# Two fully masked attentions on three-bank rings, every second unit in turned order

## What is computed

```python
# L3_attn: 16 heads of 8, 256 queries, 256 keys
attn = jnp.einsum('bhqd,bhkd->bhqk', q, k) * scale
attn = jnp.where(mask, attn, jnp.float32(-jnp.inf))
attn = jax.nn.softmax(attn, axis=-1)
out = jnp.einsum('bhqk,bhkd->bhqd', attn, v)
# L3_xattn: 16 heads of 8, 256 queries, 512 keys of the context
scores = jnp.einsum('bhqd,bhkd->bhqk', query, key_) / jnp.sqrt(D_K)
scores = jnp.where(mask == 0, NEG, scores)
attn = jax.nn.softmax(scores, axis=-1)
ctx = jnp.einsum('bhqk,bhkd->bhqd', attn, value)
```

## Time and profile before

| | us |
|---|---|
| median of 3 runs | 1503.12 (1502.01 to 1513.15) |
| the profiled execution, whole | 1489.0 |
| its span, first to last instruction | 1486.8 |
| TensorE, VectorE, ScalarE, GpSimd busy | 1200.8, 902.3, 704.1, 274.2 |
| mean granted TensorE clock, as a share of full speed | 0.885 |

### The profile page before, as it was taken

The page is one execution under the profiler, slowest core; times in us unless marked ns, Lnnn a source line. Parts: engine busy times, 40 slices in busy tenths (PEclk is TensorE's granted clock), DMA queues, the critical chain, the costliest instruction groups (busy, mean ns, idle before and its releaser), DMA issues. The chain is left out here.

```text
span 1486.8 us, 26544 instructions
## 1 busy us (share of the span) xinstructions
PE 1200.8 (81%) x9482; PEld 739.3 (50%) x9489; DVE 902.3 (61%) x2363; ACT 704.1 (47%) x1344; POOL 274.2 (18%) x549
## 2 busy tenths in 40 slices
PE   4878998687596398567999999999957679878883
PEld 2333334585243298355666666666647633333332
DVE  5747774433677445685776766766741266567746
ACT  3754774121452022212665665665714335526663
POOL 2412110353010255100000000000006513211110
PEclk9886989798799699776999999999988879969995
DMA  7321233494702466100000000000037632212100
GB/s 185 93 55 39 63 94 136 152 289 141 188 2 92 144 226 228 33 1 0 1 1 1 1 1 1 1 2 1 1 91 219 193 118 79 58 28 61 40 2 15
DMA packets 87892, 114.33 MB, mean 77 GB/s; under 512 B 10946, under 2 KB 67983, under 8 KB 87295
## 3 DMA queue, kind: packets, MB, share of 16 engines
q1 hardware_dynamic: 83314, 103.52, 23.5%
q0 software_dynamic: 4448, 9.12, 2.2%
HBM read 85.79 MB, written 25.82 MB: 75 GB/s over the span
## 5 line engine op out<-in xcount | busy, mean ns | idle before, releaser
L870 DVE TENSOR_REDUCE mx<-ps 128x4 f32<-128x1024 f32 (+1 forms) x128 | 153.9, 1221 | 58.3 <-PE ps L794 57.3
L1023 PE MATMUL ps<-probs,vaug 128*32 128x256 f32 (+1 forms) x1792 | 148.4, 406 | 15.2 <-ACT probs L989 8.6
L2508 DVE CUSTOM_DVE_ANT_0 wring<-ps,probs 128x768 f32<-128x768 f32 x128 | 122.6, 958 | 56.9 <-PE ps L2380 56.8
L2464 ACT COPY qs<-ps 128x768 f32<-128x768 f32 x128 | 102.4, 801 | 97.6 <-PE ps L2387 97.6
L979 ACT ACTIVATE probs<-ps 128x1024 f32<-128x1024 f32 x96 | 98.4, 1024 | 77.9 <-PE ps L843 77.5
L984 ACT ACTIVATE probs<-ps 128x512 f32<-128x512 f32 x192 | 106.6, 595 | 45.3 <-PE ps L937 43.6
L243 POOL TENSOR_TENSOR rstd<-veps,mhalf 128x8 f32<-128x8 f32 x12 | 19.9, 1661 | 567.2 <-DVE veps L228 536.9
L2446 ACT ACTIVATE wring<-wring,r 128x768 f32<-128x768 f32 x128 | 120.7, 943 | 2.9 <-DVE r L2511 2.9
L2387 PE MATMUL ps<-ident,wring 128*128 128x128 f32 x768 | 110.4, 281 | 3.2 <-DVE wring L2545 3.2
L794 PE MATMUL ps<-ks,qs 49*128 49x256 bf16 (+1 forms) x512 | 84.3, 370 | 27.2 <-DVE mx L865 13.8
L2387 PEld LDWEIGHTS ps<-ident,wring 128*128 128x128 f32 x768 | 84.6, 141 | 39.4 <-issue 35.3
(11 more groups left out here) (345 smaller groups left out, 2372.7 us busy)
## 6 DMA issues: line engine op xcount, KB each, us to landing
wring<-in_L_ffn_w SPq DMA_DIRECT2D x19, 768.0 KB, 6.0
wring<-in_L_ffn_w SPq DMA_DIRECT2D x32, 384.0 KB, 4.0
wring<-in_L_ffn_w SPq DMA_DIRECT2D x19, 514.0 KB, 5.6
qs<-scr_q SPq DMA_DIRECT2D x18, 192.0 KB
qs<-scr_qx SPq DMA_DIRECT2D x16, 192.0 KB
probs<-in_L_ffn_w SPq DMA_DIRECT2D x8, 384.0 KB, 4.2
probs<-in_L_ffn_w SPq DMA_DIRECT2D x4, 768.0 KB, 7.4
scr_k<-probs SPq DMA_DIRECT2D x21, 128.0 KB, 2.3
```

What stands on the lines that cost most here:

```text
L870: dve.tensor_reduce(out, src, AX.X, ALU.max, negate=True).then_inc(a_max.sem, 1)
L1023: ins = pe.matmul(ps[32 * j:32 * j + 32, self.av_bank(s), q0:S], vaug[:, s % 2, kt, j, :], probs[:, s % 2, j, at:at + S - q0], start=(kt = ...
L2464: act.copy(self.pT[:, g % 2, j, :, k * P:(k + 1) * P], self.buffer("turn", i, 0, KV).rearrange("p (t n) -> p t n", n=P)).then_inc(self.out ...
L2508: dve.tensor_tensor_reduce(self.sc[:, s, :], src, self.maskb[:, u // (2 * PR), :], 1.0, -3.0e38, ALU.add, ALU.max, self.top[:, s:s + 1]).t ...
```

## The change

The first pass gets the banks 0 to 2 as a ring, the second pass the banks 3 to 5: unit `k` takes the two banks `(2k) % 3` and `(2k + 1) % 3` of its ring. Reduces and exponentials work and count by bank, so twice as many of half the width, and TensorE waits for the first half of the unit before where it waited for whole units. In units with odd `b` the order on TensorE is turned: the value sum of the tick first, then the scores of both passes, the masks last, added on top of the scores; the unit's semaphore is raised by its last mask product. Even units keep masks, scores, value sum. In the cross-attention's odd ticks the `turn` and `oT` steps go ahead of the unit with the value sum.

```diff
@@ -181,14 +181,15 @@
     first_quad = counter("first_quad", [slices[n][0] if c["cross"] else 4 for n, c in enumerate(ATTN)], 16)
     rows_in = counter("rows_in", [4, 4], 16)
     a_mm = counter("a_mm", [G * u * m for u, m in zip(a_units, maxed)])
-    a_max = counter("a_max", [G * u * m for u, m in zip(a_units, maxed)])
+    by_bank = [2 if c["mask"] == "full" else 1 for c in ATTN]
+    a_max = counter("a_max", [G * u * m * r for u, m, r in zip(a_units, maxed, by_bank)])
     m_split = counter("m_split", [G * m for m in maxed])
     m_tp = counter("m_tp", [G * m for m in maxed])
     m_sb = counter("m_sb", [G * m for m in maxed])
     m_in = [counter(f"m_in{i}", [G // 4 * m for m in maxed], 32) for i in range(4)]
     b_mm = counter("b_mm", [G * u for u in units])
     clipped = counter("clipped", [G * u * (1 - m) for u, m in zip(units, maxed)])
-    p_exp = counter("p_exp", [G * u for u in units])
+    p_exp = counter("p_exp", [G * u * r for u, r in zip(units, by_bank)])
     va_set = counter("va_set", [G] * len(ATTN))
     av_mm = counter("av_mm", [G] * len(ATTN))
     o_sb = counter("o_sb", [G] * len(ATTN))
@@ -272,7 +273,7 @@
             self.n, self.norm, self.name, self.sub = n, norm, c["name"], c["sub"]
             self.cross, self.maximum, self.mask = c["cross"], c["maximum"], c["mask"]
             self.kt, self.u, self.nch, self.nv = kt_n[n], units[n], chunks[n], vgroups[n]
-            self.ua, self.paired = a_units[n], paired[n]
+            self.ua, self.paired, self.by_bank = a_units[n], paired[n], by_bank[n]
             self.o_bank = 7 if self.maximum else 6
             self.slots = 2 if self.maximum else 4
             self.behind = 8 if self.cross else 5
@@ -296,9 +297,9 @@
             at = (g // NQ * PAIRS + g % NQ * 2 + c) * self.keys
             return ks[HALF * r:HALF * r + rows, at + lo:at + (hi or self.keys)]
 
-        def a_bank(self, k):
-
-            return k % 2 * 2 if not self.paired or k <= self.behind - 3 else 0
+        def banks(self, first, k):
+
+            return [first + (2 * k + r) % 3 for r in range(2)]
 
         def chunk(self, i):
 
@@ -784,30 +785,33 @@
                 pe.wait_ge(rows_in.sem, rows_in.at(n // 3, 4))
             if k >= 2:
                 pe.wait_ge(a_max.sem, a_max.at(n, k - 1))
-            self.a_scores(pe, s, a, k % 2 * 2).then_inc(a_mm.sem, 1)
-
-        def a_scores(self, pe, s, a, at):
+            self.a_scores(pe, s, a, [k % 2 * 2, k % 2 * 2 + 1]).then_inc(a_mm.sem, 1)
+
+        def a_scores(self, pe, s, a, at, masked_first=False):
 
             c, tiles = (a // 2, (a % 2,)) if self.cross else (a, (0, 1))
             for i, t in enumerate(tiles):
                 for r in range(2):
-                    ins = pe.matmul(bank(at + r, i * self.keys, (i + 1) * self.keys),
+                    ins = pe.matmul(bank(at[r], i * self.keys, (i + 1) * self.keys),
                                     self.qv(s, c, r, ROWS_A, t * P, (t + 1) * P), self.kv(s, c, r, ROWS_A),
-                                    start=self.cross or not self.paired, stop=True, skip_group_check=True)
+                                    start=self.cross or not self.paired or not masked_first and i == 0, stop=self.cross or masked_first or not self.paired,
+                                    skip_group_check=True)
             return ins
 
-        def mask_tensor(self, pe, at, mask, swapped):
+        def mask_tensor(self, pe, at, mask, swapped, first):
 
             for r, lo in ((0, 0), (1, 1), (0, 1), (1, 0)):
                 rows, out = slice(HALF * r, HALF * r + HALF), slice(HALF * lo, HALF * lo + HALF)
-                pe.matmul(ps[out, at + r, :], identb[rows, rows], (mask if lo == r else swapped)[rows, :],
-                          start=True, stop=False, skip_group_check=True)
+                ins = pe.matmul(ps[out, at[r], :], identb[rows, rows], (mask if lo == r else swapped)[rows, :],
+                                start=first, stop=not first, skip_group_check=True)
+            return ins
 
         def masked_tensor(self, pe, t):
 
             n, a, b = self.n, t, t - self.behind
             maxima, exponents = a < G * self.u, 0 <= b < G * self.u
             (s, u), (e, ub) = divmod(a, self.u), divmod(b, self.u)
+            first = b % 2 == 0
             if t == 0:
                 pe.wait_ge(loaded, LOADED + 16 * 4)
             if exponents:
@@ -815,35 +819,41 @@
                 if ub == 0:
                     pe.wait_ge(m_in[e % 4].sem, m_in[e % 4].at(n, e // 4 + 1))
                 if b == 0:
-                    pe.wait_ge(a_max.sem, a_max.at(n, self.behind - 2))
                     pe.wait_ge(v_sb.sem, v_sb.at(n, 2 if self.cross else self.nv))
-                if b >= 2:
-                    pe.wait_ge(p_exp.sem, p_exp.at(n, b - 1))
+                if b >= 1:
+                    pe.wait_ge(p_exp.sem, p_exp.at(n, 2 * b - 1))
                 at = slice(kt0 * S, (kt0 + 2) * S)
                 if self.cross:
-                    self.mask_tensor(pe, 2 + b % 2 * 2, m3x[:, 1, at], m3x_half[:, at])
+                    mask_b = m3x[:, 1, at], m3x_half[:, at]
                 else:
-                    self.mask_tensor(pe, 2 + b % 2 * 2, m3a[:, 1, :], m3a_half[:, 1, :])
+                    mask_b = m3a[:, 1, :], m3a_half[:, 1, :]
+                if first:
+                    self.mask_tensor(pe, self.banks(3, b), *mask_b, True)
             if maxima:
                 if u == 0:
                     self.stack_landed(pe, s)
                 if a == 0 and n == 3:
                     pe.wait_ge(rows_in.sem, rows_in.at(1, 4))
-                if a > self.behind - 3:
-                    pe.wait_ge(a_max.sem, a_max.at(n, a))
-                elif a >= 2:
-                    pe.wait_ge(a_max.sem, a_max.at(n, a - 1))
-                if not self.cross:
-                    self.mask_tensor(pe, self.a_bank(a), m3a[:, 0, :], m3a_half[:, 0, :])
+                if a >= 1:
+                    pe.wait_ge(a_max.sem, a_max.at(n, 2 * a - 1))
+                if not self.cross and first:
+                    self.mask_tensor(pe, self.banks(0, a), m3a[:, 0, :], m3a_half[:, 0, :], True)
             if maxima:
-                self.a_scores(pe, s, u, self.a_bank(a)).then_inc(a_mm.sem, 1)
+                ins = self.a_scores(pe, s, u, self.banks(0, a), first)
+                if self.cross or first:
+                    ins.then_inc(a_mm.sem, 1)
             if exponents:
                 for t in range(2):
                     for r in range(2):
-                        ins = pe.matmul(bank(2 + b % 2 * 2 + r, t * S, (t + 1) * S),
+                        ins = pe.matmul(bank(self.banks(3, b)[r], t * S, (t + 1) * S),
                                         self.kv(e, c, r, ROWS_B, (kt0 + t) * P, (kt0 + t + 1) * P),
-                                        self.qv(e, c, r, ROWS_B), start=False, stop=True, skip_group_check=True)
-                ins.then_inc(b_mm.sem, 1)
+                                        self.qv(e, c, r, ROWS_B), start=not first and t == 0, stop=first, skip_group_check=True)
+                if first:
+                    ins.then_inc(b_mm.sem, 1)
+            if maxima and not self.cross and not first:
+                self.mask_tensor(pe, self.banks(0, a), m3a[:, 0, :], m3a_half[:, 0, :], False).then_inc(a_mm.sem, 1)
+            if exponents and not first:
+                self.mask_tensor(pe, self.banks(3, b), *mask_b, False).then_inc(b_mm.sem, 1)
 
         def a_vector(self, dve, s, a):
             n, k = self.n, s * self.ua + a
@@ -852,21 +862,26 @@
             elif a == 0 and self.prev:
                 dve.wait_ge(m_split.sem, m_split.at(n - 1, G))
             dve.wait_ge(a_mm.sem, a_mm.at(n, k + 1))
-            src = ps[:, self.a_bank(k):self.a_bank(k) + 2, :]
             if self.cross:
                 out = mx[:, s % 2, :].rearrange("p (c r t) -> p c t r", c=2, r=2)[:, a // 2, a % 2, :]
             else:
                 out = mx[:, s % 2, 4 * a:4 * a + 4]
-                src = src.rearrange("p r (t k) -> p (r t) k", t=2)
             if self.mask == "full" and self.cross:
                 if k >= 2:
-                    dve.wait_ge(a_max.sem, a_max.at(n, k - 1))
+                    dve.wait_ge(a_max.sem, a_max.at(n, 2 * (k - 1)))
                 for r in range(2):
-                    ins = dve.tensor_tensor_reduce(wring[:, k % 2, r * S2:(r + 1) * S2], src[:, r, :],
-                                                   m3x[:, 0, a % 2 * S2:(a % 2 + 1) * S2], 1.0, -3.0e38,
-                                                   ALU.add, ALU.max, out[:, r:r + 1])
-                ins.then_inc(a_max.sem, 1)
+                    dve.tensor_tensor_reduce(wring[:, k % 2, r * S2:(r + 1) * S2], bank(self.banks(0, k)[r]),
+                                             m3x[:, 0, a % 2 * S2:(a % 2 + 1) * S2], 1.0, -3.0e38,
+                                             ALU.add, ALU.max, out[:, r:r + 1]).then_inc(a_max.sem, 1)
```

(55 more changed lines are left out.)

## The result

The changed kernel takes 1523.41 us (median of 4 runs, 1521.37 to 1525.37), the kernel before, run beside it, 1507.55 us (4 runs, among them the three of the table before). These medians are 15.9 us (1.05%) apart. By either number the kernel is slower, by 1 to 2%; the prediction had +10.4 us (0.7%) and called "within 1%" the likeliest. The mechanism that it named is what the trace shows. In the stages that the change touches, the loss is nearly twice the sum.

The account below looks back on a forecast made before the run. VectorE's loop over the maxima was taken as the bound, replaced by a wait for the exponential. Terms 3.9 + 2.0 + 3.7 + 0.8 gave +10.4 us: 1499.4 on the profiled execution, 1513.5 on the 1503.1 median; range 1494 to 1528.

Parts of the forecast that it names:

- What bounds before: Both attention stages: VectorE's loop over the maxima sets the pace, 1.80 us a cross unit where TensorE alone needs 1.44.
- The wait that takes its place: Between odd and even units' masks, TensorE waits for the odd exponential's first half: 1.12 us between starts, 0.88 of it idle.
- The plain cross group: Cross stage: four units, all on TensorE's chain, take 7.69 us against 7.41, +0.28; fourteen groups cost +3.9 us.
- The switch from Sb to M: Odd units, exponents' scores to masks: taken as 0.33 us because a tiling change drains TensorE; otherwise 0.11 shorter a pair.
- Rival B: Whole kernel: cheaper switches, exponents' scores to masks and value sum to maxima's scores, plus VectorE's relief cancel the loss: 1498; chance 0.25.
- A: Both stages: TensorE runs free, the exponential wait being small, cross -21 us and self -7: 1475 us; chance 0.10.
- AV to Sa: Odd units, value sum to scores of the maxima: 0.57 us, taken from the value-sum-to-masks spacing before.
- The self group: Self stage: two units take 4.53 us against 4.22, twelve groups +3.7; next stage's work priced at 0, bounds -4 and +4.
- A group has two of these, and one `o_tp` ..., and one `turn` ...: Cross group sum: two pairs of 3.55 us, plus 0.50 for value-sum transposes and 0.09 for maxima transposes, 7.69 in all.
- Hidden at nothing: the units before the first exponents: Units ahead of the first exponents: priced at no cost, because VectorE sets their pace before and after the change.
- Rival C: Both stages: 0.9 us of idle time in every pair lowers TensorE's clock, +27 us in a quarter of pairs: 1540; chance 0.10.
- The chances: Whole kernel, about 1% being tellable from no change: faster 0.08, same 0.62, slower 0.30; the forecast itself 0.55.

Follow-up runs that it names:

- The kernel that opens VectorE's loop alone: The kernel before, with the cross stage's one pair of banks for the maxima handed over by halves: ratio 0.9933, and 0.9887 when run again.
- The two experiments that ran in two groups: Kernel before with only exponentials and self-stage reductions halved: 1.0052, then 0.9983. Kernel before with cross-stage maxima banks handed over by halves: 0.9933, then 0.9887.

## Why the prediction was right, and where it was not

**What bounds before: right.** The kernel that opens VectorE's loop alone gains 8.9 us in M(b8) to M(b56), the 9.1 us of waiting that stood there.

**The wait that takes its place: right, place and size.** M to M from odd to even was worked out as 1.12 us; it is 1.11 in one pair of a group and 1.20 in the other (idle 0.87 and 0.96 by the prediction's reckoning, M to M less 0.24, for 0.88 worked out; the brackets have 0.70 and 0.80, as they count from the end of the matmul's fill), released by the exponential each time, and no wait for VectorE is left in the steady part. The 0.09 us by which the two pairs differ arise behind the exponential: its start (0.46 behind M) and its first half (0.60) are alike in both, and the next M follows 0.05 us behind that half in one and 0.14 in the other. The later one is, in every case, the first unit of a group, where the same M also waits for `m_in`, which had come 2.2 us earlier or more. That this second wait costs the 0.09 us was not tested apart.

**The plain cross group: right.** 7.76 us for 7.69. The switch from Sb to M, which the trace before didn't have, took 0.31 to 0.32 us (1404.30 to 1404.62), near the 0.33 assumed; M to Sa 0.34 to 0.35, like-to-like 0.22. The rule of the Trainium skill on a change of tiling mode (TensorEngine Tiling (Array Packing), Key Properties), by which the prediction said that the switch drains, agrees with the trace here as far as starts can tell: about 0.1 us more than between like ones. Rival B, which needed it to be gone, falls with it, and so does A: the idle time is 0.87 to 0.96 in every pair, where A wanted less than 0.74 to gain at all. AV to Sa is 0.57 as taken.

**The self group: right, and the stage too high.** A group takes 4.57 us in the steady part for 4.53. The window b4 to b28 gained 2.5 us on the prediction's 3.7; within the plus or minus 4 set for the next stage's work. From the timeline of TensorE, the counterpart of the earlier trace rows:

```profile
1261.99 0.40 PE L805 MATMUL ps<-m3a,identb 64*64 64x512 bf16 x2 [0.58 <-ACT probs L995]
...
1262.21 0.41 PE L805 MATMUL ps<-m3a,identb 64*64 64x512 bf16 x2
...
1262.55 0.39 PE L795 MATMUL ps<-ks,qs 49*128 49x256 bf16 x4
```

**The step that failed: "A group has two of these, and one `o_tp` ..., and one `turn` ...", times fourteen.** Every fourth group also holds oT and the next one y, and the sum has neither. Before, they cost 0.37 and -0.16 us, lying in VectorE's slack; on a chain "with no slack left" (the prediction's own words) they cost 0.57 and 1.11. M(b8) to M(b56) holds three groups with oT and two with y: 0.6 and 2.5 us. The sum was low by 0.08 in each of the twelve groups as well, 1.0 us. The first three groups, b8 to b20, cost 1.0 us more than that, because the first holds the last query projection and the second a gap of 0.56 us ahead of its value sum whose cause the profile doesn't show. Together 5.1 us, what separates 8.4 from 3.3. The rows are the query projection (0.63 us between the starts around it, where it had VectorE's slack before), oT and y, and the `turn` behind y:

```profile
1364.96 0.70 PE L409 MATMUL ps<-hT,w 128*128 128x256 f32 x2
...
1394.83 0.44 PE L1097 MATMUL ps<-ident,o 128*128 128x128 f32 x2
...
1398.40 0.71 PE L1119 MATMUL ps<-w,oT 128*128 128x128 f32 x4
...
1399.83 0.27 PE L921 MATMUL ps<-identb,mpart 128*12 128x128 bf16 x2
```

Both bring a wait with them. oT needs the last division of VectorE (L1083, done at 1394.78), so it starts 0.76 us behind AV, not 0.57. y adds 0.77 between two AVs; `turn`, which writes to the same bank 7, must then wait until VectorE has added y to `x` (L1129, done at 1399.57), and starts 0.79 behind AV, not 0.45. Moving the jobs into the gap gave it back, and more (88.56 us for 98.39). What the text noted for `o_tp`, that a job behind slack before is on the path now, had to be asked of each job in the order.

**The other failed step: "Hidden at nothing: the units before the first exponents", and what lies between the stages.** The sum went over the two steady windows and their tails alone. The ends outside them cost 0.7 us at the self stage's start, 3.3 from M(b28) to the cross stage (4.1 less the 0.8 of the tail) and 0.7 at the cold start of the cross stage beyond what its groups explain: 4.7 us. With the 5.1 above, 0.7 more in the cross tail and 1.2 less in the self window, that is the 9.3 us between 10.4 and 19.7. The largest of the ends, 2.1 us, has a row. The last unit of the self stage is a turned one, so its exponential starts late and the copy of the value sums queues behind two halves of it. The wait of 0.86 us there before is 1.50 after, and the clock falls behind it:

```profile
1320.67 0.90 PE L1038 MATMUL ps<-probs,vaug 128*32 128x256 f32 x8 [1.50 <-ACT osb L1055]
...
1326.16 1.23 PE L1119 MATMUL ps<-w,oT 128*128 128x128 f32 x4 [0.46 <-ACT oT L1107]
```

```profile
1319.20:1328.93 9.73, 5.13 (x26) 2.19 (x27) 2.32 (x12) 2.10 (x5) 0.00 (x0) 0.59 0.02 7
```

The same steps take 7.67 us before, at a granted clock of 0.92, with an output product of 0.71 us for 1.23.

**Rival C, the clock: not in the steady part, but at an end.** The granted clock is 1.00 in M(b8) to M(b56) with 0.7 to 0.8 us of waiting in every pair. The rule of the Trainium skill on short idle times between groups of matmuls (TensorE: Matmul & The Clock Gate, A second HAM failure mode) is not borne out at that size. One argument against C was misread: the waits before are not "as long in sum", they are 9.1 us for 18.0. The clock held all the same. Waits of 1.2 to 1.5 us brought the clock down in some places and not in others (above).

**The chances.** With all that M(b8) to M(b56) held, the forecast would have been 5.1 us higher, 1518.6 us, just over one per cent; with the 4.7 us of the ends well beyond it. The case for "slower" was put down to delays on ScalarE and a costlier switch. The switch was not costlier, and the steady part shows no such delay; one came at the end of the self stage (the 1.50 us above). So 1523.41 us lies within the stated 1494 to 1528 in part by luck: the upper end was set for other reasons, and 4.4 us of the time are the base, 1507.55 in place of 1503.12. A smaller slip: by the earlier trace rows TensorE is busy for 88 to 96% of the four windows, not 83.

## What to carry to other kernels

When a change takes the last slack from an engine's loop, list every job in the engine's order, the rare ones of the batch too, and price each at its full length on the new chain, with the wait for whatever must empty the bank that it shares. Before turning an order to save switches, draw the spacing of each engine's own instructions over the whole period: two bunched value sums made one side of the pair short, and any loop longer than that side put an uncovered wait there. Where one engine's buffer is the bound, hand the buffer over by halves and put other work between the halves, before taking a bank from a neighbour that will then wait at the cold start.

## What was not expected of the hardware

- The part ahead of these stages, the same code in every kernel here, took from 1214.5 to 1238.8 us, and it goes by group: 1214.5 to 1218.9 in the first, 1229.0 to 1236.8 in the second, 1232.3 to 1238.8 in the third. The medians of the kernel before go the same way (1481.16, 1501.21, 1506.01), and the first two groups ran on one chip, so it isn't the chip alone. The two experiments that ran in two groups had ratios of 1.0052 and 0.9983, and 0.9933 and 0.9887: both lower by 0.5 to 0.7% in the third group; whether that is the chip or the group is open. Effects under half a per cent are better read from the steady windows than from ratios: M(b8) to M(b56) agreed to less than 0.2 us in each of the three kernels profiled twice, whole stages only to 0.0, 2.1 and 2.7.
- A mask group that had one wait began 0.05 us behind the end of the instruction that released it, and one with a second wait, satisfied 2.2 us or more earlier, 0.14 or 0.15 behind, in each of the 12 cases of either kind in M(b8) to M(b56) of the changed kernel. Nothing else was varied to single the second wait out.
- Waits of TensorE of the same size don't always lower its clock: one of 1.4 us a group left it at 1.00 in some groups and at 0.83 on average in four others; 1.2 to 1.3 us in every pair left it at 1.00 but for 3.5 us in 111. In two executions of the changed kernel the self stage had one late transfer of the same 2.1 us; M(b4) to M(b28) had a granted clock of 0.97 in one and 0.90 in the other. What tells the cases apart is open.
